# Wide attention of a four-layer attention and expert kernel: semaphores that count upward, another order within a step, and a norm spread over steps

## The reference, cut to what matters

```
ik, mk = input_seq @ Wk + bk, state_seq @ Wk + bk
iv, mv = input_seq @ Wv + bv, state_seq @ Wv + bv
q = einsum('bmd,hdp->bhmp', state_seq, Wq) + bq
inp_score  = einsum('bhmp,bsp->bhms', q, ik)
self_score = sum(q * mk[:, None], axis=-1, keepdims=True)
attn  = softmax(concatenate([self_score, inp_score]) / sqrt(128))
heads = einsum('bhms,bsp->bhmp', attn[..., 1:], iv) + attn[..., 0:1] * mv[:, None]
x1  = layernorm(heads_flat @ Wo + bo + state_seq) * g1 + b1
mlp = relu(x1 @ Wg + bg) * (x1 @ Wl + bl) @ Wm + bm
return layernorm(mlp + x1) * g2 + b2
```

## Time and profile before

| | us |
|---|---|
| median of 3 runs | 954.55 |
| lowest and highest | 954.46, 960.34 |
| the profiled execution | 962.13 |
| its span, first to last instruction | 960.4 |
| mean granted clock of PE | 0.831 of full |
| busy: PE, PEld, DVE, ACT, POOL | 82%, 68%, 60%, 43%, 42% |

### The profile page before, as it was taken

One profiled execution on the slowest core, in us unless ns is written; L12 is line 12 of the kernel. 1 busy time (PEld: TensorE's weight loads), 2 busy tenths in 40 slices (PEclk: granted clock), 3 DMA queues, 4 the chain that ended last, 5 costly groups with the idle time before them and its releaser, 6 DMA issues. The chain is left out here.

```text
span 960.4 us, 15537 instructions
## 1 busy us (share of the span) xinstructions
PE 786.4 (82%) x4650; PEld 648.7 (68%) x4650; DVE 575.0 (60%) x1494; ACT 416.8 (43%) x1275; POOL 400.2 (42%) x374
## 2 busy tenths in 40 slices
PE   4888489999899998897739999667854999997665
PEld 2565379998788787785628788445634888886654
DVE  5555565445677777675464777647654546666444
ACT  1745044444244444343204677267621446654211
POOL 4542322211554543331221577388535048875100
PEclk9555779999789999898768999755576999999578
DMA  6000001110000000000002335000001032210000
GB/s 236 2 1 1 23 12 45 44 55 12 1 2 1 1 8 1 1 1 1 2 16 61 123 134 179 1 0 2 1 1 47 9 123 91 74 44 1 0 1 23
DMA packets 14285, 33.18 MB, mean 35 GB/s; under 512 B 1744, under 2 KB 5864, under 8 KB 13952
## 3 DMA queue, kind: packets, MB, share of 16 engines
q1 hardware_dynamic: 14208, 32.26, 10.0%
HBM read 31.63 MB, written 0.62 MB: 34 GB/s over the span
## 5 line engine op out<-in xcount | busy, mean ns | idle before, releaser
L1229 PE MATMUL banks<-input_hi,weights_in_lo 128*128 128x512 f32 x296 | 126.0, 426 | 26.8 <-PEq L1511 13.9
L1229 PE MATMUL banks<-input_lo,weights_in_hi 128*128 128x512 f32 x296 | 121.3, 410 | 0.0
L1229 PE MATMUL banks<-input_hi,weights_in_hi 128*128 128x512 f32 x296 | 120.8, 408 | 0.0
L989 ACT ACTIVATE probabilities<-banks,neg_max 128x128 f32<-128x128 f32 x256 | 89.8, 376 | 60.9 <-ACTq L986 60.9
L1229 PEld LDWEIGHTS banks<-weights_out,hidden 128*128 128x128 f32 x864 | 100.9, 192 | 3.2 <-DVE hidden L2268 1.0
L1229 PE MATMUL banks<-weights_out,hidden 128*128 128x128 f32 x864 | 101.6, 276 | 0.7 <-ACT att_feat L1142 0.7
L694 POOL TENSOR_TENSOR rstd<-var_eps,neg_half 128x4 f32<-128x4 f32 x24 | 25.0, 1042 | 176.5 <-POOLq L693 156.8
L1060 ACT ACTIVATE probabilities<-banks,neg_max 128x128 f32<-128x128 f32 x128 | 45.2, 365 | 100.8 <-ACTq L1058 100.8
L1089 ACT ACTIVATE hidden<-banks,cols 128x512 f32<-128x512 f32 x80 | 54.6, 688 | 78.0 <-ACTq L1087 77.9
L1229 PEld LDWEIGHTS banks<-input_hi,weights_in_lo 128*128 128x128 f32 x296 | 59.3, 200 | 41.2 <-issue 29.4
L877 POOL TENSOR_TENSOR scratch<-values_state,self_weight 128x512 f32<-128x512 f32 x32 | 33.3, 1040 | 96.6 <-POOLq L865 81.9
(11 more groups left out here) (264 smaller groups left out, 1858.7 us busy)
## 6 DMA issues: line engine op xcount, KB each, us to landing
scratch<-cw_rows SPq DMA_DIRECT2D x19, 512.0 KB, 3.9
weights_out<-w_in SPq DMA_DIRECT2D x17, 256.0 KB, 3.0
weights_in<-w_in SPq DMA_DIRECT2D x8, 512.0 KB, 3.6
weights_in<-w_in SPq DMA_DIRECT2D x9, 256.0 KB, 3.2
weights_in<-w_in SPq DMA_DIRECT2D x16, 128.0 KB, 2.1
weights_out<-w_in SPq DMA_DIRECT2D x16, 128.0 KB, 2.1
wq<-w1q_in SPq DMA_DIRECT2D x1, 1024.0 KB, 4.8
wo<-w1o_in SPq DMA_DIRECT2D x1, 1024.0 KB, 6.9
```

The costliest lines, as they stand in the source:

```text
L989: act.activation(prob[:, n // 2 % 2, h, :], b8(n % 3)[:, i, :], ACT.Exp, bias=neg_max8[:, n % 4, i:i + 1], accum_out=z[:, n // 2 % 2, h:h ...
L1229: return pe.matmul(o, l, rh, start=start, stop=stop, **kw)
```

## The change

Semaphores of this stage count upward: nobody takes them back, waits are for n + 1 (or 4 (n + 1), 5 (n + 1)), an instruction increments the one semaphore that all its readers wait for, and the waits of an engine for itself in front of increments go. Semaphores that only said that a buffer is free again go too, where another wait implies it. The order and the lags of the stages on each engine change. The first half's norm is cut into `statistics`, `variance`, `centre` and `scale`, each for two batches a step (the variance for four), in steps 23 to 32. Ahead of the stage, the projections of values are made in halves around the transposes.

```diff
@@ POOL
-                pipelined(pool, [(lambda it, n: inverse_roots((0,)), (15,), 8), (self_values, range(32), 2),
-                                 (self_products, range(32), 0),
-                                 (lambda it, n: low_heads(wq1, wq_hi, wq_lo, 1, 2), (1,), 0),
-                                 (lambda it, n: low_heads(wo1, wo_hi, wo_lo, 0, 3), (2,), 0),
-                                 (lambda it, n: low_heads(wo1, wo_hi, wo_lo, 1, 4), (4,), 0),
-                                 (add_row, (6, 8), 0), (mlp_weights, (12, 14, 16, 18), 0)],
+                pipelined(pool, [(lambda it, n: inverse_roots((0,)), (15,), 12), (self_values, range(32), 4),
+                                 (self_products, range(32), 1),
+                                 (lambda it, n: low_heads(wo1, wo_hi, wo_lo, 0, 3), (3,), 0),
+                                 (lambda it, n: low_heads(wq1, wq_hi, wq_lo, 1, 2), (5,), 0),
+                                 (lambda it, n: low_heads(wo1, wo_hi, wo_lo, 1, 4), (7,), 0),
+                                 (add_row, (9, 11), 0), (mlp_weights, (12, 14, 16, 18), 0)],
@@ ACT
                     act.activation(self_exp[:, n % 2, :], self_arg[:, n % 2, :], ACT.Exp)\
-                        .then_inc(st.sem, st.one())
-                    act.wait_ge(st.sem, st.n)
-                    act.sem_inc(probs_ready, 1)
-                    act.sem_inc(probs_ready_dve, 1)
...
-                pipelined(act, [(round_headsT, range(32), 5), (copy_probsT, range(32), 3),
-                                (copy_sums, (15, 31), 6), (exps, range(32), 1)], 32, 1, st.close)
+                pipelined(act, [(take_tokens, (1,), 0), (evacuate_state_keys, (1,), 0),
+                                (round_headsT, range(32), 5), (copy_probsT, range(32), 3),
+                                (exps, range(32), 2), (copy_sums, (15, 31), 6)], 32, 1, st.close)
@@ PE
+                def self_scores(it, n):
+                    if n > 0:
+                        pe.wait_ge(wide_max_ready, n)
+                    pe.wait_ge(qmk_ready, n + 1)
+                    for i in range(4):
+                        at = 4 * (n % 2) + i
+                        m = mm(bank[7][:, at:at + 1], qmk[:, n % 2, i, :], ones[:, :])
+                    m.then_inc(wide_scores_done, 1)
...
                 def turn(it, n):
-                    pe.wait_ge(probs_ready, 1)
-                    pe.sem_inc(probs_ready, -1)
+                    pe.wait_ge(wide_probs_ready, 5 * (n + 1))
                     if n == 20:
                         pe.wait_ge(y_read, 1)
-                        pe.sem_inc(y_read, -1)
...
-                pe.sem_inc(q_free, 1)
-                pipelined(pe, [(queries, range(32), 0), (state_rest, (0,), 0), (scores, range(32), 1),
-                               (output, range(32), 6), (values, range(32), 3), (turn_sums, (15, 31), 7),
-                               (turn_heads, range(32), 4), (turn, range(32), 2)],
-                          32, 1, lambda: None)
+                pipelined(pe, [(queries, range(32), 0), (turn_state, (0,), 0), (self_scores, range(32), 1),
+                               (output, range(32), 6), (turn_heads, range(32), 4), (values, range(32), 3),
+                               (turn_sums, (15, 31), 7), (turn, range(32), 2), (scores, range(32), 0),
+                               (state_rest, (0,), 1)], 32, 1, lambda: None)
...
+            project_tok(w("wv1"), ctxT, 6, (0,))
             transpose_half(0, xn, 4)
-            project_tok(w("wv1"), ctxT, 6)
-            transpose_half(1, xn, 5)
-            pe.wait_ge(keys_ready, 1)
-            pe.sem_inc(keys_ready, -1)
+            project_tok(w("wv1"), ctxT, 6, (1,))
+            pe.wait_ge(keys_ready, 2)
@@ DVE
                 def queries(it, n):
-                    dve.wait_ge(heads_q_done, 1)
-                    dve.sem_inc(heads_q_done, -1)
+                    dve.wait_ge(heads_q_done, n + 1)
                     dve.tensor_scalar(scratch[:, n % 2, :], bank[0][:, :], col("bq1", n % 16), None, ALU.add)\
-                        .then_inc(st.sem, st.one())
-                    dve.wait_ge(st.sem, st.n)
-                    dve.sem_inc(qh_ready, 1)
-                    dve.sem_inc(qh_ready_pool, 1)
-                    dve.sem_inc(q_free, 1)
+                        .then_inc(qh_ready, 1)
...
                     dve.scalar_tensor_tensor(self_arg[:, n % 2, :], own, SC1, neg_max[:, n % 8, :],
-                                             ALU.mult, ALU.add).then_inc(st.sem, st.one())
-                    dve.wait_ge(st.sem, st.n)
-                    dve.sem_inc(neg_max_ready, 1)
-                    dve.sem_inc(own_free, 1)
+                                             ALU.mult, ALU.add).then_inc(wide_max_ready, 1)
...
+                def centre(it, b):
+                    dve.wait_ge(st.sem, st.n)
+                    for i in (b, b + 1):
+                        dve.scalar_tensor_tensor(att[:, i, :], att[:, i, :], mean_var[:, i, 0:1], row("g1"),
+                                                 ALU.subtract, ALU.mult).then_inc(st.sem, st.one())
...
-                pipelined(dve, [(heads_out, range(32), 4), (queries, range(32), 0), (state_values, (0,), 0),
-                                (low_headsT, range(32), 5), (weights, range(32), 2), (maxima, range(32), 1),
-                                (residual, (15, 31), 7),
-                                (lambda it, n: norm_stats(0, att, 1e-6), (15,), 8),
-                                (lambda it, n: norm_apply(0, att, xm, norm_tok_ready, "g1", lambda b: row("be1")),
-                                 (15,), 9)], 32, 1, st.close)
+                pipelined(dve, [(low_headsT, range(32), 5), (heads_out, range(32), 4), (weights, range(32), 3),
+                                (queries, range(32), 0), (state_values, (0,), 2), (maxima, range(32), 1),
+                                (second_tokens, (0,), 2), (residual, (15, 31), 7),
+                                (statistics, (0, 2), 23), (variance, (0,), 26), (centre, (0, 2), 27),
+                                (scale, (0, 2), 30)], 32, 1, st.close)
...
             norm_stats(1, x, 1e-5)
+            split_input(0)
             norm_apply(1, x, xn, norm_tok_ready)
-            split_input(0)
             copy_values(iv, 6, "bv1")
-            dve.wait_ge(st.sem, st.n)
-            dve.sem_inc(qkv_ready, 1)
```

225 lines of the change are left out of this document (100 added, 125 removed).

## The result

The changed kernel takes **923.14 us** (median of 4 runs, 922.02 to 924.19) against 954.5 (954.45 to 960.34): ratio 0.966, 95% interval 0.962 to 0.970. The profiled execution of the changed kernel took 922.02 us, span 920.3, mean granted clock 0.846.

The account below looks back on a forecast made before the run. DVE's queue was taken as the bound of the wide attention, PE next at 4.95 us a step. Terms -19.3 - 4.8 - 5 - 5 = -34, less 2 for the slow profiled execution: 954.55 - 32 = 922.5 us, range 912 to 938.

Parts of the forecast that it names:

- the four stretches: DVE's idle times of 0.44, 0.26, 0.47 and 0.26 us in each wide-attention step, together 1.43.
- the first rival: DVE idles because the engine empties itself, not for semaphores; steps stay 5.77 us, total 944.5; chance 0.07.
- Counting upward, and the order: -19.3: Wide attention, steps 6 to 31: 25 steps fall from 5.77 to 5.0 us; bounds -11.8 and -20.5.
- DVE's need, 4.5: DVE's time per wide-attention step after counting upward: 4.33 us of work plus 0.2 for remaining waits.
- beside other work: Claim that PE, ACT and POOL also lose signalling instructions, but alongside other work; no size given.
- a ring for the new order (3.7): Heads turned on PE, rounded on ACT, low part and outputs on DVE: 3.3 us at most plus some 0.4, under 4.95.
- Norm: -4.8: Steps 22 to 25: spreading the norm removes the 7.3 us excess, 2.5 stays; bounds -7.3 and -1.
- Start: -5: Stage start: first eviction 3.0 us earlier, first six steps 2 us shorter; bounds 0 and -8.
- End: -5: Stage end: last products with ones 3.3 us closer to last queries, chain behind 1.5 shorter; bounds -2 and -7.
- The signs: Listed profile marks: evictions 4.95 to 5.1 us apart, one PE residual wait; wrong if 5.7 or DVE awaits rounding each step.
- two or three spells of 4 us: PE falls to 1.2 GHz in the residual's step or the fill: 932 to 936 us; chance 0.12.
- The slower rival: DVE's idle stretches stay and the new order adds a 0.6 us rounding wait per step: 965 us; chance 0.04.

Follow-up runs that it names:

- e1: Kernel before, old order, with only DVE's signals in the wide attention counting upward (their readers wait for the counters): 943.0 us, ratio 0.982.
- e5: e1 with ACT's exponentials counting upward too (ACT's wait for itself and two increments removed), still old order: 933.5 us, ratio 0.974.
- e2: Changed kernel with DVE's four waits for itself, seven increments and six decrements a step put back: 962.7 us, ratio 1.003 to the kernel before.
- e3: Changed kernel with only DVE's four waits for its own last instruction put back, no increments or decrements: 930.2 us.
- e4: Changed kernel with only DVE's increments and decrements put back, without waits for itself: 927.4 us.
- e10: Changed kernel with DVE's waits for itself and increments put back, but without the decrements: 943.2 us.
- e7: Changed kernel with the maximum written to PSUM bank 7 and `neg_max` made from there: 921.7 us.
- e9: Changed kernel with ACT's wait for its own exponentials and two increments put back: 922.8 us.
- e8: e7 plus POOL's inverse roots one step later and PE's key products ahead of the turned probabilities: 919.0 us, ratio 0.960 to the kernel before.
- e6: Changed kernel with the first half's norm in one piece again (statistics and variance in one step, centre and scale in the next): 926.7 us.

## Why the prediction was right

**The bound.** Right, and e1 with e5 show it by itself: DVE's queue held the step at 5.77, and what held it were the four stretches. The sentence "they stand exactly where DVE waits for its own last instruction and then does semaphore increments by hand" is confirmed by e2, e3, e4 and e10: neither half alone lengthens the step (4.93 and 4.95); both together bring back 1.32 us of idle stretches in e2 and a quiet step of 5.65. The Trainium skill, page "VectorE: DVE Perf Modes", section "The DRAIN you can't avoid", on which the first rival leaned, compared a chain of copies with a semaphore after each to one with a semaphore at its end. No run here has such a chain; the nearest is e3, whose waits for the instruction's own increment put the next start 0.04 behind the end, against 0.08 before it without a wait (e4). The section does not speak of increments as commands of their own, and those are what the prediction's first term rests on.

**Counting upward, and the order: -19.3.** From step 6 to 31, 152.4 us became 125.6: -26.8. The sixteen without the norm fell by 15.2, the full length of the other nine by 7.3: 22.5 for this term. The step came out at 4.85 on average in the sixteen, under the 5.0 that I took, since seven ran at 4.68: there DVE was still catching up with PE, whose own steps (first query product to first query product) took 4.93 to 4.96 from step 7 to 22. Two numbers behind the term were wrong without touching it. DVE's need, 4.5, is 3.96 by its work (e7), where independent operations start before the one in front ends, and 4.68 with `neg_max` held; all three lie under PE's 4.95. And I left ACT "beside other work": in the old order its 0.27 was in the ring (e1 to e5, 0.32 a step). It did no harm to the sum only because the new order takes it off the path (e9). I had worked out a ring for the new order (3.7) and never looked for that of the old one (5.26).

**Norm: -4.8.** The nine steps from 22 held 7.7 over nine full ones and now hold 3.4: -4.3. The residual costs 1.5, as forecast; the 1.4 in step 27 was not forecast: "POOL's inverse roots meet a variance that is ready" was wrong. The roots stand at the head of POOL's list and the variance at the end of DVE's in the step before; the weights for POOL's next product were done at 371.24, the variance only at 373.76, and all of POOL's work stood behind it. e8 mends it. By e6 the spread itself is worth 2 to 4 of time, as DVE now has room to catch up; with DVE's bound gone, the norm in one piece would have cost less than the 7.3 that I counted.

**Start: -5.** First eviction 243.18 against 246.20 (-3.0, as forecast), step 6 another -1.8 (forecast -2). That both agree is in part luck, for the clock differs too. The kernel before ran at 0.50 in 240 to 244 us and again in 260 to 264, which the prediction left out of the start. e5, in the old order, kept 1.00 in 236 to 248: its first eviction came at 244.58, 1.6 earlier than before, and its step 6 at 271.44, earlier than in the changed kernel. So how much of the start the new order itself brought is open.

**End: -5.** From the last eviction to the MLP 29.9 became 23.9: -6.0. The last products with ones stand 5.0 behind the last queries, as forecast; from the last queries to the last output it is -6.1. From there to the MLP, where I had expected no change, 8.45 became 7.00.

**The sum.** Forecast -34 in the profile, less 2; measured -26.8 - 4.9 - 6.0 = -37.7 to the MLP, -40.1 in all, of which 2.4 lie behind the stage in code that nothing touched, and -31.4 between the medians. The profiled execution before was 7.6 over its median, and I took 2 of it off; about 8.7 was due. So the forecast is within 0.7 us by two errors of 6 to 7 us with opposite signs, which is luck. The start of the sum was uncertain by as much: three of the four runs behind 954.5 lay within 0.1 of each other, but in the later 31 the medians were 958.4 to 959.6, and beside those e9, as fast as the changed kernel, is 36.6 below the kernel before (959.3 to 922.8). The mechanism is right; by these later times the change is worth some 4.6 us more than the forecast gave it.

**The signs.** The evictions, the distance of steps 22 and 25 (16.33), the clock, the first eviction and the last output came as listed. Two signs did not. PE has a second wait, 1.25 for POOL, besides the residual's 0.87. And DVE does wait for the rounding, 0.16 to 0.23 us in seven of the steps from 15 to 24, which was named as a sign of being wrong; it costs nothing, because it lies inside the slack that DVE has under PE's 4.96. Three sums in the rivals and chances do not close either, without touching the forecast: the first rival's terms give 944.75 and not 944.5, two or three spells of 4 us on 922.5 give 930.5 to 934.5 and not 932 to 936, and 0.77, 0.12 and half of 0.07 are already 0.92 to 0.93 and not 0.91.

**The slower rival**, the new order with the stretches kept, is e2: 962.7 where I had written 965, but only 0.3% over the kernel before on the same chip. Its mechanism does not show: the low part waits 0.36, no longer than the commands in front of it explain; what adds is the held `neg_max`. No kernel here has the new order with the old signalling on all engines.

## What to carry to other kernels

Where an engine waits for its own instruction and then increments by hand, every command behind that wait stands on its path: let the instruction increment one counter that only rises, and let each reader wait for its own count. Before crediting an order with a gain, change the signalling alone in the old order: here that gave 2.6% (e5) where the whole change gives 3.4 to 3.7% (the changed kernel and e9), and the new order with the old signalling on DVE gave none. When one bound goes, follow the ring of the next from instruction to instruction over all engines; an engine that is "beside other work" in one order is in the ring in another.

## What was not expected of the hardware

**A short DVE operation is held by POOL.** `neg_max` (TENSOR_SCALAR, 128x4, source and target in SBUF) takes 0.17 us alone, 0.9 in the changed kernel's steps of 4.68, 0.6 in those of 4.96 and up to 1.68, and ends within 0.03 us of the POOL operation beside it (342.30 and 342.28); with its source in PSUM it was 0.16 in all 32 steps (e7). The operations around it in the same steps, among them the 128x4 maximum with one operand in PSUM, stay at 0.16. The Trainium skill, page "SBUF — State Buffer", section "Who interferes with whom", states it: such an operation can enter a mode that takes the port pair shared with GpSimd, and whoever comes second waits for the whole instruction of the other. The trace agrees; I had not weighed it, and in the kernel before it mostly hid: there `neg_max` ran from 298.05 to 298.22 in a typical step, and POOL's value product ended at 298.16. Once in its fill it stood there to be read:

```profile
268.03 1.27 POOL L867 TENSOR_TENSOR scratch<-scratch,queries_feat 128x512 f32<-128x512 f32 x1
...
268.42 0.90 DVE L2070 TENSOR_SCALAR neg_max<-row_max 128x4 f32<-128x4 f32 x1
```

Nor is it this operation alone: the 128x4 addition `exp_sums`, with both sources in SBUF, takes 1.30 us in place of 0.16 in two steps of e7, from 263.32 to 264.62, beside a POOL operation that ends at 264.60.

**Signalling commands are free or dear by place**: 0.09 us each behind a wait for oneself, nothing to be seen behind a 0.75 us operation without one.

**One idle stretch can cost twice, or not.** PE's clock was 0.50 for eight us in e3's fill and 0.60 for four in e7, behind a wait of 1.25 us; behind the same 1.25 us it stayed at 1.00 in the changed kernel. What decides between the two is not shown here. With the wait for the roots gone, and 0.9 of the residual's, the last eviction came 3.7 us earlier from e7 to e8.
